# Attention on one NeuronCore: where V's product stands in the first step of a unit

## The chip, the cores and the metric

The kernel runs on one core of one Trainium2 chip. The metric is the device time in microseconds of one execution; three runs of the kernel before are shown. A profile covers one further execution. TensorE, ScalarE (ACT), VectorE (DVE), GpSimd (POOL) and SyncE (SP) run their own instruction streams and meet at semaphores.

## What is computed

```python
xn = _layernorm(x)                       # x: 2 x 1024 x 256, f32
x = x + attention(xn) + moe_ffn(xn)      # 8 experts, top 2

# attention: 16 heads of 16, 4 key heads
scores = einsum('bhqd,bhkd->bhqk', Qr, Kr) / HEAD_DIM ** 0.5
weights = softmax(scores, axis=-1)
out = einsum('bhqk,bhkd->bhqd', weights, V_rep)
return out.transpose(0, 2, 1, 3).reshape(b, s, d) @ W_o
```

All 1024 keys are seen by every query. Q and K are projected and turned by rope, the K heads are repeated four times over the query heads.

## The kernel before, in words

The first 170 us are the layer norm, the routing, the projections and the experts. Then comes the attention, in 16 units. A group g (0 to 7) is a batch and a key head; its unit u = 2 * g + h takes half h of the queries (512) for the four query heads of that key head. A unit has KT = 8 steps, kt = 0 to 7, one for each block of 128 keys.

For each step three streams work beside each other:

- **Scores, exponentials, V.** TensorE computes the scores of the next step (kt + 1) in two halves, j = 0 and j = 1, of two heads each (`scores`, L1338, matmuls at L1352; at kt = 0 of a unit a product that subtracts the maxima at L1348 goes ahead). Each half has one bank pair of PSUM, so half j of the next step waits until ScalarE has taken the exponential of half j of this step (`exp_done`). ScalarE's exponentials are at L785, two for each step, and each waits for its half (`st_ready`). V's product (`values`, L1356, matmuls at L1362) waits for both exponentials of its step and adds into the output bank over the eight steps. At kt = 0 it also waits for `o_free`: VectorE's transposition of that bank, L1080, which is issued after the maxima of the unit before.
- **Maxima of unit u + 2.** For the softmax of two units later TensorE computes four products of q and k for each step. Two go first, on rows 0 to 63 and 64 to 127 of the array (`score_first`, L1231 and L1233). The high keys' product (`score_high`, L1241) and the low keys' product (`score_low`, L1248) come later. ScalarE copies the result of L1231 out as the gain (`take_gain`, L736), in its queue behind the two exponentials of the step, and `score_low` waits for it, since it overwrites the bank. VectorE takes maxima: `take_a` (L992), `take_high` (L997) and `take_low` (L1003, merges the gain).
- **Side work.** VectorE transposes and inverts finished units (L1080, L1084, L1090) and prepares the maxima (L1009 to L1028). GpSimd divides (L649), mixes the experts' rows, and stages V (`stage_v`, L614). SP loads keys, queries and maxima for later groups.

Products on 64 rows are written out in pairs, a low one (rows 0 to 63) and a high one, which run beside each other. The order of TensorE is by hand. For steps 1 to 6, `values_between` (L1367) splits V into its first 128 and the other 384 query columns and puts two pairs between: scores half j = 1 of heads part 0 with `score_high`, then `score_low` with part 1. These are called the third and the fourth pair below; the first is `score_first` (the maxima pair), the second the scores of j = 0. For step 0, `values_behind` (L1376) puts third and fourth pair together and V whole behind them. Step 7 (L1444 to L1459) issues the scores of the next unit, `score_high` and `score_low`, and V whole. The last group (g = 7) has no maxima to compute and has a path of its own.

ScalarE's order in a step is: exponential j = 0, exponential j = 1, gain.

```python
def exps(u, first=False, ahead=True):
    for kt in range(KT):
...
        for j in range(2):
            act.wait_ge(st_ready, 2 * s + j + 1)
            act.activation(probs[kt % 2][:, 2 * j:2 * j + 2, :].rearrange("p r q -> p (r q)"),
                           st_ps[j][:, :], ACT.Exp, scale=1.0 / math.sqrt(HD)).then_inc(exp_done, 1)
        if ahead:
            take_gain(u + 2, kt)
```

Of the kernel before, what the change touches and what calls it, by code (L numbers as in the profile page):

```python
# [35 lines left out]
def build(nc, x, w_q, w_k, w_v, w_o, w_r, w_g, w_u, w_d, cos_t, sin_t, out):  # L36
# [3 lines left out]
    KV = w_k.shape[1] // HD  # L40
    R = NH // KV
    E, _, F = w_g.shape
    NT = B * S // P
    ST_T = S // P
# [27 lines left out]
    with ExitStack() as ctx:  # L72
# [297 lines left out]
        def max_bank(v, i):  # L370

            return first_mx_ps[i % 4] if v < 2 else mx_ps[(NI * v + i) % 3]
# [5 lines left out]
        def taken(v, n):  # L378

            return NTAKEN * v + n  # L380

        def key_block(kt):

            return kt // QT * QT + (3, 1, 2, 0)[kt % QT]
# [767 lines left out]
        def _(pe):  # L1152
# [72 lines left out]
            def score_first(v, q, p, k):  # L1225

                i, j, rows = 4 * k, k // QT, slice(k % QT * P, (k % QT + 1) * P)
                if v or k:
                    pe.wait_ge(mx_taken, taken(v, 3 * k - 1))
                low, high = max_bank(v, i), max_bank(v, i + 1)  # L1230
                mm(low.rearrange("p (c n) -> p c n", c=2), qs[q][0:STACK, j, rows], ka[p][0:STACK, :, QUART:HALF],  # L1231
                   start=True, stop=True).then_inc(mx_scored, 1)
                mm(high.rearrange("p (c n) -> p c n", c=2), qs[q][STACK:P, j, rows], ka[p][STACK:P, :, 0:QUART],  # L1233
                   start=True, stop=True).then_inc(mx_scored, 1)

            def score_high(v, q, p, k, waited=False):

                i, j, rows = 4 * k + 2, k // QT, slice(k % QT * P, (k % QT + 1) * P)
                if (v or k) and not waited:
                    pe.wait_ge(mx_taken, taken(v, 3 * k))  # L1240
                mm(max_bank(v, i).rearrange("p (c n) -> p c n", c=2), qs[q][STACK:P, j, rows], ka[p][STACK:P, :, QUART:HALF],  # L1241
                   start=True, stop=True).then_inc(mx_scored, 1)

            def score_low(v, q, p, k):

                i, j, rows = 4 * k + 3, k // QT, slice(k % QT * P, (k % QT + 1) * P)
                pe.wait_ge(gain_ready, STEPS * v + k + 1)
                mm(max_bank(v, i).rearrange("p (c n) -> p c n", c=2), qs[q][0:STACK, j, rows], ka[p][0:STACK, :, 0:QUART],  # L1248
                   start=True, stop=True).then_inc(mx_scored, 1)

            def score_second(v, q, p, k, waited=False):
                if (v or k) and not waited:
                    pe.wait_ge(mx_taken, taken(v, 3 * k))
                pe.wait_ge(gain_ready, STEPS * v + k + 1)
                score_high(v, q, p, k, True)
                score_low(v, q, p, k)
# [81 lines left out]
            def scores(q, v, p, kt, s, j, banks=None, parts=(0, 1)):  # L1338
                if s is not None and parts[0] == 0:
                    pe.wait_ge(exp_done, 2 * (s - 1) + j + 1)  # L1340
                out = [st_ps[j][:, i * HALF:(i + 1) * HALF] for i in range(2)]
                half = [slice(STACK * i, STACK * (i + 1)) for i in range(2)]

                first = ((0, 2, 3, 1), (3, 1, 2, 0))[kt // QT][kt % QT]
                keys = slice(first * P, (first + 1) * P)
                if kt == 0:
                    for i in parts:
                        mm(out[i], ones_r[half[i], :], ms[v][half[i], j, :], start=True, stop=False)  # L1348
                for i in parts:
                    if i == 1 and banks is not None:  # L1350
                        pe.wait_ge(mx_taken, banks)
                    last = mm(out[i], kb[p][half[i], kt // QT, keys], qs[q][half[i], j, :], start=False, stop=True, skip_group_check=kt > 0)  # L1352
                if parts[-1] == 1:
                    last.then_inc(st_ready, 1)

            def values(p, kt, s, u, columns=slice(0, HALF)):  # L1356
                if columns.start == 0:
                    pe.wait_ge(exp_done, 2 * (s + 1))
                    if kt == 0:
                        pe.wait_ge(o_free, u + 1)  # L1360
                for r in range(R):
                    last = mm(o_ps[32 * r:32 * (r + 1), columns], v_st[p][:, key_block(kt), :], probs[kt % 2][:, r, columns],  # L1362
                              start=(kt == 0 and columns.start == 0), stop=(kt == KT - 1), skip_group_check=True)
                if columns.stop == HALF:
                    last.then_inc(products_done, 1)

            def values_between(q, kv, p, kt, s, u, score):  # L1367

                values(p, kt, s, u, slice(0, P))
                scores(q, kv, p, kt + 1, s + 1, 1, None, (0,))  # L1370
                score_high(*score)
                score_low(*score)
                scores(q, kv, p, kt + 1, s + 1, 1, None, (1,))
                values(p, kt, s, u, slice(P, HALF))

            def values_behind(q, kv, p, s, u, score):  # L1376

                scores(q, kv, p, 1, s + 1, 1, None, (0,))
                score_high(*score)
                score_low(*score)  # L1380
                scores(q, kv, p, 1, s + 1, 1, None, (1,))
                if u % 2 == 0:
                    pe.wait_ge(v_staged, u // 2 + 1)
                values(p, 0, s, u)

            pe.wait_ge(kb_loaded[0], 128)
            pe.wait_ge(m_loaded[0], 64)
# [24 lines left out]
            def project(n, kt):  # L1412
                jobs = [(t, c) for t in out_tiles(n) for c in range(KC)]
                for t, c in jobs[len(jobs) * kt // KT:len(jobs) * (kt + 1) // KT]:
                    project_tile(t, [c])

            def group(g, p, last):
                for h in range(2):
                    u = 2 * g + h
                    ahead = 2 * (1 - p) + h  # L1420

                    for kt in range(KT):
                        s = KT * u + kt
                        if not last:
                            if kt == 0:
                                pe.wait_ge(q_loaded[ahead], 64 * ((g - p) // 2 + p) + 64)
                                if h == 0:
                                    pe.wait_ge(ka_loaded[1 - p], 128 * ((g - p) // 2 + p) + 128)
                            score_first(u + 2, ahead, 1 - p, kt)
                        if kt == KT - 1 and h == 0:  # L1430
                            pe.wait_ge(m_loaded[1], 64 * (g + 1))
                        if kt == KT - 1 and h == 1 and not last:
                            pe.wait_ge(kb_loaded[1 - p], 128 * ((g - p) // 2 + p) + 128)
                            pe.wait_ge(m_loaded[0], 64 * (g + 2))


                        if kt < KT - 1 and not last:
                            scores(2 * p + h, h, p, kt + 1, s + 1, 0)
                            if kt == 0:
                                values_behind(2 * p + h, h, p, s, u, (u + 2, ahead, 1 - p, kt))  # L1440
                            else:
                                values_between(2 * p + h, h, p, kt, s, u, (u + 2, ahead, 1 - p, kt))
                            continue
                        for j in range(2):  # L1444

                            free = taken(u + 2, 3 * kt) if j == 1 and not last else None
                            if kt < KT - 1:
                                scores(2 * p + h, h, p, kt + 1, s + 1, j, free)
                            elif h == 0:
                                scores(2 * p + 1, 1, p, 0, s + 1, j, free)  # L1450
                            elif not last:
                                scores(2 * (1 - p), 0, 1 - p, 0, s + 1, j, free)
                        if not last:
                            score_second(u + 2, ahead, 1 - p, kt, True)
                        if last:
                            project(h, kt)
                        if h == 0 and kt == 0:
                            pe.wait_ge(v_staged, g + 1)
                        values(p, kt, s, u)  # L1459

            for g in range(G):
                group(g, g % 2, g == G - 1)
# [37 lines left out]
```

## Time and profile before

| | us |
|---|---|
| median of three runs | 502.73 |
| lowest and highest | 502.05, 502.80 |
| the profiled execution, its own time | 502.22 |
| its span, first to last instruction | 500.3 |

The page gives the busy time of each engine, the granted TensorE clock (tenths of full speed, nine in all 40 slices, which is 90% or more; the mean over the core is 1.000), and the chain of work that ended last. The attention runs from about 171 to 492 us. Its steps are read in the timeline: start, duration, engine, line, operation, and in brackets the idle time of the engine before the row with what ended it. PE is TensorE's matmuls. The distance between the starts of two groups is a better measure of TensorE than the durations, as the ends are modelled.

### The profile page before, as it was taken

What the parts mean: (1) busy time and instruction counts of PE and PEld (TensorE: products, weight loads), DVE (VectorE), ACT (ScalarE), POOL (GpSimd) and SP (SyncE); (2) the same over time, 40 slices, a digit from 0 to 9 for tenths busy, and PEclk for the clock granted to TensorE, in tenths of its full rate; (3) what the DMA queues carried; (4) which work ended last, traced back from release to release, by engine and by line L of the source; (5) the groups of instructions that cost most, each with busy time, mean ns of one, the idle gap of its engine ahead of it and who ended that gap; (6) DMA issues with size and microseconds to landing.
All of it is one profiled execution on the core that took longest, in us unless ns stands there. A gap on an engine that the chain in (4) does not pass through costs nothing.

```text
span 500.3 us, 10998 instructions
## 1 busy us (share of the span) xinstructions
PE 490.1 (98%) x3952; PEld 266.7 (53%) x3952; DVE 371.7 (74%) x874; ACT 407.3 (81%) x551; POOL 172.2 (34%) x214
## 2 busy tenths in 40 slices
PE   7999999999999999999999999999999999999997
PEld 7836999888888633433333334333333343334433
DVE  4683867977876578788888887888888888884124
ACT  2646766665665699999999999999999999997772
POOL 5007677544521002241551426513454235400000
PEclk9999999999999999999999999999999999999999
DMA  8992467754573123122133024113223312001101
GB/s 286 370 313 62 111 208 233 205 174 154 135 208 88 66 66 87 42 65 88 45 88 104 24 68 137 32 45 98 76 63 88 86 44 61 27 3 33 43 33 63
DMA packets 41428, 52.76 MB, mean 105 GB/s; under 512 B 9792, under 2 KB 27584, under 8 KB 41376
## 3 DMA queue, kind: packets, MB, share of 16 engines
q1 hardware_dynamic: 29152, 34.36, 23.1%
q0 software_dynamic: 3408, 9.31, 7.2%
q10 hardware_dynamic: 8816, 8.40, 5.0%
q8 instruction: 32, 0.52, 0.4%
q14 instruction: 20, 0.16, 0.1%
HBM read 36.18 MB, written 15.60 MB: 104 GB/s over the span
## 4 chain that ended last, share of the span: by engine, by line
PE 94%; ACT 3%; DVE 2%; DMA 1%; issue 0%; ACTq 0%
PE bank L1362 28%; PE bank L1352 15%; PE bank L1292 14%; PE bank L1231 10%; PE bank L1302 7%; PE bank L1248 5%; PE bank L1407 3%; PE bank L1192 3%; PE bank L1284 2%; PE bank L1270 2%; ACT xn_t L736 2%; PE bank L1348 2%; PE bank L1181 1%; DMA xs<-in_L_attn_x 1%; PE bank L1196 1%; PE bank L1166 1%
## 5 line engine op out<-in xcount | busy, mean ns | idle before, releaser
L785 ACT ACTIVATE big<-bank 128x1024 f32<-128x1024 f32 x256 | 247.9, 1025 | 10.1 <-PE bank L1352 10.1
L1362 PE MATMUL bank<-big,v_st 128*32 128x384 f32 (+2 forms) x1696 | 154.3, 436 | 0.0
L1352 PE MATMUL bank<-qs,kb 64*128 64x512 f32 x512 | 133.9, 419 | 0.7 <-ACT big L785 0.7
L997 DVE TENSOR_REDUCE mx<-bank 128x1 f32<-128x512 f32 x128 | 87.9, 687 | 28.7 <-PE bank L1241 21.0
L992 DVE TENSOR_REDUCE mx<-bank 128x1 f32<-128x512 f32 x128 | 87.8, 686 | 15.6 <-PE bank L1233 13.5
L736 ACT ACTIVATE xn_t<-bank 128x512 f32<-128x512 f32 x128 | 76.4, 597 | 21.6 <-PE bank L1270 14.4
L1003 DVE CUSTOM_DVE_ANT_0 xn_t<-bank,xn_t 128x512 f32<-128x512 f32 x128 | 87.3, 682 | 0.0
L1352 PEld LDWEIGHTS bank<-qs,kb 64*128 64x128 f32 x512 | 63.9, 184 | 33.9 <-issue 16.7
L1292 PE MATMUL bank<-xn,work 128*128 128x128 f32 x624 | 76.0, 275 | 0.0
L1292 PEld LDWEIGHTS bank<-xn,work 128*128 128x128 f32 x624 | 72.9, 192 | 0.6 <-issue 0.5
L1362 PEld LDWEIGHTS bank<-big,v_st 128*32 128x32 f32 x1696 | 33.4, 108 | 68.8 <-issue 35.6
L649 POOL TENSOR_TENSOR xn<-xn,rden 128x256 f32<-128x256 f32 x15 | 9.5, 635 | 159.6 <-DVE rden L1084 144.4
L1231 PEld LDWEIGHTS bank<-ka,qs 64*128 64x128 f32 x112 | 20.5, 183 | 75.5 <-DVE mx L997 63.7
L1231 PE MATMUL bank<-ka,qs 64*128 64x512 f32 x112 | 55.4, 495 | 0.0
L1233 PE MATMUL bank<-ka,qs 64*128 64x512 f32 x112 | 55.3, 494 | 0.0
L1241 PE MATMUL bank<-ka,qs 64*128 64x512 f32 x112 | 52.9, 472 | 0.0
L1248 PE MATMUL bank<-ka,qs 64*128 64x512 f32 x112 | 45.7, 408 | 2.8 <-ACT xn_t L736 2.8
L569 POOL DMA_INDIRECT xn<-xn_d,token_of x39 | 40.2, 1030 | 20.2 <-PE bank L1284 13.0
L713 ACT ACTIVATE work<-big 128x1024 f32 x39 | 41.2, 1056 | 4.7 <-DVE slot_ei L979 2.9
L1302 PE MATMUL bank<-big,xn 128*128 x156 | 40.5, 382 | 0.3 <-DVE xn L1048 0.2
L634 POOL TENSOR_SCALAR rope_a<-rope_a,gate 128x256 f32<-128x256 f32 x32 | 29.3, 921 | 32.2 <-DMA rope_a<-rows_out,place_i 32.2
L1048 DVE SCALAR_TENSOR_TENSOR xn<-xn,bank 128x256 f32<-128x256 f32 x39 | 16.3, 419 | 31.4 <-ACT xn L749 31.3
(151 smaller groups left out, 534.3 us busy)
## 6 DMA issues: line engine op xcount, KB each, us to landing
qs<-q_hl SPq DMA_DIRECT2D x64, 128.0 KB, 2.8
rows_out<-xn ACTq DMA_DIRECT2D x37, 128.0 KB, 2.8
ka<-k_hl SPq DMA_DIRECT2D x64, 64.0 KB
kb<-k_hl SPq DMA_DIRECT2D x64, 64.0 KB
xs<-in_L_attn_x SPq DMA_DIRECT2D x4, 512.0 KB, 6.4
big<-in_L_ffn_Wg SPq DMA_DIRECT2D x16, 128.0 KB, 6.5
big<-in_L_ffn_Wu SPq DMA_DIRECT2D x16, 128.0 KB, 6.6
big<-in_L_ffn_Wd SPq DMA_DIRECT2D x16, 128.0 KB, 6.5
```

Source lines behind the costliest of these rows:

```text
L736: act.activation(gain[k % 2], max_bank(v, 4 * k), ACT.Relu).then_inc(gain_ready, 1)
L785: act.activation(probs[kt % 2][:, 2 * j:2 * j + 2, :].rearrange("p r q -> p (r q)"), st_ps[j][:, :], ACT.Exp, scale=1.0 / math.sqrt(HD)).t ...
L992: nc.vector.reduce_max(mx[h][:, STEPS + k, 0:1], max_bank(v, i), axis=X_AXIS).then_inc(mx_taken, 1)
L997: nc.vector.reduce_max(mx[h][:, STEPS + k, 1:2], max_bank(v, i), axis=X_AXIS).then_inc(mx_taken, 1)
L1003: nc.vector.tensor_tensor_reduce(larger, max_bank(v, i), gain[k % 2], scale=1.0, scalar=-FAR, op0=ALU.add, op1=ALU.max, accum_out=mx[h][:, ...
L1231: mm(low.rearrange("p (c n) -> p c n", c=2), qs[q][0:STACK, j, rows], ka[p][0:STACK, :, QUART:HALF], start=True, stop=True).then_inc(mx_sc ...
L1233: mm(high.rearrange("p (c n) -> p c n", c=2), qs[q][STACK:P, j, rows], ka[p][STACK:P, :, 0:QUART], start=True, stop=True).then_inc(mx_scor ...
L1248: mm(max_bank(v, i).rearrange("p (c n) -> p c n", c=2), qs[q][0:STACK, j, rows], ka[p][0:STACK, :, 0:QUART], start=True, stop=True).then_i ...
L1292: last = mm(gu_ps[i % 2][:, f * P:(f + 1) * P], w_now[i % 2][:, c, f * P:(f + 1) * P], rows_t[i % 2][:, c, :], start=(c == 0), stop=(c == ...
L1302: last = mm(y_ps[i % 2] if y is None else y, act_h[i % 2][:, c * P:(c + 1) * P], wdn[:, e, c, :], start=(c == 0), stop=(c == C - 1))
L1352: last = mm(out[i], kb[p][half[i], kt // QT, keys], qs[q][half[i], j, :], start=False, stop=True, skip_group_check=kt > 0)
L1362: last = mm(o_ps[32 * r:32 * (r + 1), columns], v_st[p][:, key_block(kt), :], probs[kt % 2][:, r, columns], start=(kt == 0 and columns.sta ...
```

## The change

Only the order in TensorE's stream at kt = 0 of the 14 units of groups 0 to 6 changes. V goes, whole, behind the third pair and ahead of the fourth, and the wait for the staged V goes with it. The function is renamed.

```diff
-            def values_behind(q, kv, p, s, u, score):
+            def values_within(q, kv, p, s, u, score):
 
                 scores(q, kv, p, 1, s + 1, 1, None, (0,))
                 score_high(*score)
-                score_low(*score)
-                scores(q, kv, p, 1, s + 1, 1, None, (1,))
                 if u % 2 == 0:
                     pe.wait_ge(v_staged, u // 2 + 1)
                 values(p, 0, s, u)
+                score_low(*score)
+                scores(q, kv, p, 1, s + 1, 1, None, (1,))
...
-                                values_behind(2 * p + h, h, p, s, u, (u + 2, ahead, 1 - p, kt))
+                                values_within(2 * p + h, h, p, s, u, (u + 2, ahead, 1 - p, kt))
```

## Rows read from the trace of the kernel before

**Rows 1.** The page: engine shares, and the chain that ended last by engine.
```profile
PE 490.1 (98%) x3952; PEld 266.7 (53%) x3952; DVE 371.7 (74%) x874; ACT 407.3 (81%) x551; POOL 172.2 (34%) x214
...
PE 94%; ACT 3%; DVE 2%; DMA 1%; issue 0%; ACTq 0%
```

**Rows 2.** Timeline of a regular step: start us, us, engine, line, operation, [idle before].
```profile
302.80 0.50 PE L1231 MATMUL bank<-ka,qs 64*128 64x512 f32 x1
303.14 0.39 PE L1352 MATMUL bank<-qs,kb 64*128 64x512 f32 x2
303.46 0.42 PE L1362 MATMUL bank<-big,v_st 128*32 128x128 f32 x8
303.81 0.50 PE L1352 MATMUL bank<-qs,kb 64*128 64x512 f32 x1
304.15 0.39 PE L1248 MATMUL bank<-ka,qs 64*128 64x512 f32 x1
304.48 0.85 PE L1362 MATMUL bank<-big,v_st 128*32 128x384 f32 x8
304.73 1.03 ACT L785 ACTIVATE big<-bank 128x1024 f32<-128x1024 f32 x1
305.26 0.49 PE L1231 MATMUL bank<-ka,qs 64*128 64x512 f32 x1
```

**Rows 3.** Timeline of a last step (kt = 7), TensorE alone.
```profile
311.23 0.40 PE L1352 MATMUL bank<-qs,kb 64*128 64x512 f32 x2
311.47 0.40 PE L1248 MATMUL bank<-ka,qs 64*128 64x512 f32 x1
311.80 1.07 PE L1362 MATMUL bank<-big,v_st 128*32 128x512 f32 x8
```

**Rows 4.** Timeline of the first step of the next unit, all engines.
```profile
311.26 1.94 ACT L785 ACTIVATE big<-bank 128x1024 f32<-128x1024 f32 x2
312.80 0.50 PE L1231 MATMUL bank<-ka,qs 64*128 64x512 f32 x1
313.11 0.71 DVE L1080 STREAM_TRANSPOSE xn<-bank 128x512 f32<-128x512 f32 x1
313.13 0.63 PE L1352 MATMUL bank<-qs,kb 64*128 64x512 f32 x3
313.25 0.18 PEld L1352 LDWEIGHTS bank<-qs,kb 64*128 64x128 f32 x1 [0.16 <-ACT big L785]
313.33 0.60 ACT L736 ACTIVATE xn_t<-bank 128x512 f32<-128x512 f32 x1
313.37 0.39 PE L1241 MATMUL bank<-ka,qs 64*128 64x512 f32 x1
313.82 1.94 ACT L785 ACTIVATE big<-bank 128x1024 f32<-128x1024 f32 x2
313.98 0.49 PE L1248 MATMUL bank<-ka,qs 64*128 64x512 f32 x1 [0.21 <-ACT xn_t L736]
314.40 1.06 PE L1362 MATMUL bank<-big,v_st 128*32 128x512 f32 x8
314.41 0.68 DVE L997 TENSOR_REDUCE mx<-bank 128x1 f32<-128x512 f32 x1
315.40 0.49 PE L1231 MATMUL bank<-ka,qs 64*128 64x512 f32 x1
315.43 0.69 DVE L1003 CUSTOM_DVE_ANT_0 xn_t<-bank,xn_t 128x512 f32<-128x512 f32 x1
315.93 0.60 ACT L736 ACTIVATE xn_t<-bank 128x512 f32<-128x512 f32 x1 [0.17 <-PE bank L1233]
316.06 0.42 PE L1362 MATMUL bank<-big,v_st 128*32 128x128 f32 x8
```

**Rows 5.** The gain copy (L736): who waited for it, us and times.
```profile
  PEld bank L1248: 7.3, 14
```

**Rows 6.** Timeline: TensorE's first row of another unit, four units earlier.
```profile
232.76 0.50 PE L1231 MATMUL bank<-ka,qs 64*128 64x512 f32 x1
```

## The prediction, made before the change was run

> **What bounds the kernel now.** I read the page first: engine shares and the chain that ended last [rows 1]. TensorE is busy 98% and carries 94% of the chain, most of it at the lines of the attention, ScalarE 81%, VectorE 74%. The granted clock is full in nearly every slice. That says TensorE, but the ends of matmuls are modelled, so a wait shorter than the overlap hides in a busy share. So the next view is the timeline of a regular step (kt from 1 to 6), read by the starts of TensorE's groups [rows 2]: first maxima pair 302.80, next pair j=0 303.14, V on 128 columns 303.46, third pair 303.81, fourth 304.15, V on 384 columns 304.48, next step 305.26. The distances 0.34, 0.32, 0.35, 0.34, 0.33, 0.78 add up to the step's 2.46 us.
>
> Is there a wait inside them? The pitch of V is 1.00 us for 512 columns (311.80 to 312.80) [rows 3, 4], 0.78 for 384 and 0.35 for 128: 0.22 for the first 128 columns removed and 0.43 for the next 256, so 0.22 per 128 columns and about 0.13 fixed. It grows evenly with the columns, so none of these is a wait. Pairs that follow each other stand 0.24 apart (311.23, 311.47) [rows 3]; the first pair after V takes 0.34 to the next, the last pair before V 0.33. Regular steps therefore run at TensorE's own pace. ScalarE follows with little room: two exponentials start 0.91 apart (1.94 for both [rows 4], 1.03 for one [rows 2]), and the gain copy takes 0.49 to the next start (313.33, 313.82) [rows 4]; 0.91 + 0.91 + 0.49 = 2.31 against 2.46.
>
> **The first step of a unit** (kt = 0) takes 2.60 (312.80 to 315.40) [rows 4], and there is a hole: the third pair starts at 313.37, the fourth at 313.98, 0.61 later instead of 0.24. It waits for ScalarE's gain, which itself started at 313.33, 0.53 after the maxima pair. The wait view has it 14 times, once for each unit that is not in the last group [rows 5]. This is what the edit goes for: it puts V (1.00 us) into that hole.
>
> **The change part by part.** Nothing is added or removed: V's matmuls, the two products, every semaphore count and DMA remain. V goes ahead of the fourth pair (the low keys' product, and the second half of the scores for kt = 1, j = 1). Three consequences.
>
> (1) The gain wait goes. The gain is done at 313.33 + 0.60 = 313.93, before the fourth pair can now come.
>
> (2) V waits for something else. It needs the exponentials of its step (end 311.26 + 1.94 = 313.20: there) and the free output bank, released by VectorE's transposition of the unit before, 313.11 + 0.71 = 313.82 [rows 4]. TensorE could start V at 313.37 + 0.33 = 313.70. From the end of a releasing instruction to the load it releases is 0.05 (exponential 313.20, load 313.25 [rows 4]), so V starts at 313.87: a new wait of 0.17. Bounds: 0 if V's wait overlaps otherwise, 0.27 if VectorE's release takes 0.1 more. I take 0.17, as the nearest release row says. The transposition itself does not move: it is queued on VectorE behind the unit before. The wait for the staged V costs nothing: staging is two groups ahead, with a whole group as cover (two units of 20.0 us, as below). Were it late, all of TensorE would stand, with the fourth pair now behind it.
>
> (3) The fourth pair comes late, and with it the second half of the scores for the next step. It starts at 313.87 + 1.00 = 314.87 instead of 313.98: 0.89 later. Who waits for it: ScalarE's second exponential of kt = 1. From the first pair after V to the ScalarE instruction that waits for it is 0.53 (315.40 to 315.93, a row marked as a wait for TensorE) [rows 4]. So it starts at 315.40 instead of 314.73, ends 1.03 later at 316.43, and V of kt = 1, which needs both exponentials, starts at 316.43 + 0.05 = 316.48. Before it started at 316.06 [rows 4]. **The unit is 0.42 longer.**
>
> The same from the slacks: the second exponential could have started at 313.98 + 0.53 = 314.51 and started at 315.76 - 1.03 = 314.73, slack 0.22; it ended at 315.76, plus 0.05 is 315.81 against V at 316.06, slack 0.25. Together 0.47 of cover for a shift of 0.89; 0.42 is left.
>
> TensorE's own pace would have V of kt = 1 earlier: after 314.87 come pairs at 315.21 and 315.45, V at 315.77. It then idles 0.71 for ScalarE, more than the 0.37 of the hole and its exposed load of 0.09 that went.
>
> What else moves: VectorE's merge with the low keys began at 315.43 and now could from 315.40, so it is covered, though by 0.03 only; a tenth more would delay the next maxima by as much, and they have spare time until the following maxima pair. The first maxima pair of kt = 1 comes at 315.21 and needs the high keys' maximum (314.41 + 0.68 + 0.05 = 315.14): free. No DMA and no work of SP or GpSimd is passed; their triggers (counts of score groups and products) shift by fractions of a microsecond beside transfers issued many steps ahead.
>
> Is 0.42 given back later in the unit? ScalarE has 0.15 spare per step, but the delay was already handed to TensorE at V of kt = 1, and TensorE has none: its step is the sum of its pitches. Continued: the gain starts 0.91 after 315.40, at 316.31, the next exponentials 0.49 later at 316.80 and end 1.94 later at 318.74; V of kt = 2 wants them at 316.48 + 2.46 = 318.94 by TensorE's pace. So TensorE paces again after a single step, and all engines are 0.42 late. The last step (kt = 7) shows no hole [rows 3] and hands over the same relative times, so the amount returns in each unit.
>
> The first unit has no unit before it to transpose; I price it like the others, 0.17 at most wrong. Units repeat: four take 80.04 (232.76 [rows 6] to 312.80 [rows 4]). So **14 x 0.42 = 5.9 us**. The last group has other code and only shifts.
>
> The profiled execution took 502.22 (span 500.3), 0.5 under the median 502.73; with 5.9 it gives 508.1, and the median forecast is 502.73 + 5.9 = **508.6**. The unit period goes from 20.0 to 20.4.
>
> **Where a rule of the skill stands.** The first pair after V and the last before it cost 0.10 and 0.09 more than the 0.24 of pairs in a row [rows 2, 3]. The edit makes a run of three pairs behind V (fourth pair, maxima pair, next pair), but the run ahead of V gets shorter by one: the number of V blocks is the same, so no such extra cost goes. The Trainium skill, "TensorEngine Tiling (Array Packing)", Key Properties, says that changing the tiling mode drains the engine; by that rule alone the edit would be worth nothing, since the changes of mode are as many as before. The trace agrees with the extra cost at each change, but has two other terms, the hole and the late scores.
>
> A second one bears on reading. The busy share of 98% shows neither the 0.61 nor the coming 0.71 as what they are. The Trainium skill, "Perfetto Trace Analysis", in the note that opens the page, calls matmul busy time a bad metric because matmuls are pipelined; the trace agrees, 0.61 between two starts appears as 0.21 idle [rows 4].
>
> **The rivals.**
> A, faster: only TensorE's instruction stream counts. Then V of kt = 1 stands at 315.77 instead of 316.06, 0.29 less, 14 x 0.29 = 4.1: 498.6. It needs the fourth pair to be late without cost, that is, shifted by no more than 0.47. For it: TensorE's 94% of the chain. Against: V alone puts 1.00 between the third and fourth pairs, where they stood 0.61 apart, and the second exponential's order in ScalarE's queue is fixed. Chance 0.05.
> B, no change: only changes of mode count, or ScalarE's 0.15 per step takes the delay back before TensorE feels it. For it: the spare time exists. Against: the wait falls in the very next step, before any can be taken back. 502.7, chance 0.04.
> C, slower by less: the bank is free when V wants it. V 313.70, all else 0.17 earlier: 0.25 per unit, 14 x 0.25 = 3.5: 506.2. Against: the transposition's end at 313.82. Chance 0.09.
> D, slower by more: the releases of V and of the exponential each take 0.1 longer than the rows I took them from, or VectorE's merge slips and its later maxima carry it: 0.62 per unit, 8.7: 511.4. Chance 0.08.
> My forecast has 0.74.
>
> **How the numbers follow.** 0.2% (about 1 us) is what a measurement of this kernel can tell from no change. Slower holds the forecast, C and D: 0.91; faster A: 0.05; same B: 0.04. The range runs from just below C (506.2 less 0.4, half of what the three runs shown span) to just short of D: 505.8 to 511.0; outside are A, B and most of D.
>
> **What would show it.** In the changed kernel: V of kt = 0 some 0.50 after the third pair, released by VectorE's transposition; the fourth pair 1.00 after V; a new idle time of ScalarE before the second exponential of kt = 1, of some 0.56 (315.40 less the end of the first, 313.82 + 1.02), 14 times; TensorE's V of kt = 1 starting 1.6 after the fourth pair, where pace alone gives 0.9; regular steps still 2.46. I am wrong if V's pitch there is well under 1.00, if the second exponential isn't late, or if the unit's period is 20.0 or less.

## The result: 7.5 us slower, and the profile after

| | before | after |
|---|---|---|
| median, five runs each | 502.73 | 510.19 |
| lowest and highest | 502.05, 502.80 | 509.70, 510.44 |
| profiled execution, span | 500.3 | 507.9 |

The ratio is 1.0153, with a 95% interval from 1.0143 to 1.0164: slower by 7.5 us, where 5.9 was forecast; 510.19 lies inside the range. On a further chip, told at the end of the experiments, the kernel before itself takes 511.3 us and the changed one 511.9: there the ratio is 1.0013.

The page of the changed kernel, shares and chain:

```profile
PE 487.7 (96%) x3952; PEld 266.7 (53%) x3952; DVE 372.6 (73%) x874; ACT 407.3 (80%) x551; POOL 171.7 (34%) x214
...
PE 86%; DVE 6%; ACT 4%; issue 3%; DMA 1%; DVEq 0%; ACTq 0%
```

Against [rows 1] TensorE's busy time is 2.4 us less over a span 7.6 longer, and its part of the chain falls from 94% to 86%. The other 8 points went to VectorE (2% before, 6% now: the transposition and the merge ahead of it), to time in which the profile shows no wait ("issue", 0% and 3%) and to ScalarE (3% and 4%): two waits have come into the chain. The timeline of a first step of the changed kernel, in the order of [rows 4] (the transposition's row is VectorE's):

```profile
316.69 0.50 PE L1231 MATMUL bank<-ka,qs 64*128 64x512 f32 x1
...
317.01 0.71 DVE L1080 STREAM_TRANSPOSE xn<-bank 128x512 f32<-128x512 f32 x1
...
317.27 0.39 PE L1241 MATMUL bank<-ka,qs 64*128 64x512 f32 x1
...
317.72 1.02 ACT L785 ACTIVATE big<-bank 128x1024 f32<-128x1024 f32 x1
317.84 0.19 PEld L1362 LDWEIGHTS bank<-big,v_st 128*32 128x32 f32 x8 [0.51 <-issue]
317.87 1.06 PE L1362 MATMUL bank<-big,v_st 128*32 128x512 f32 x8 [0.21 <-DVE xn L1080]
...
318.87 0.49 PE L1248 MATMUL bank<-ka,qs 64*128 64x512 f32 x1
...
319.20 0.39 PE L1231 MATMUL bank<-ka,qs 64*128 64x512 f32 x1
...
319.40 0.69 DVE L1003 CUSTOM_DVE_ANT_0 xn_t<-bank,xn_t 128x512 f32<-128x512 f32 x1
319.43 1.02 ACT L785 ACTIVATE big<-bank 128x1024 f32<-128x1024 f32 x1 [0.69 <-PE bank L1352]
319.43 0.40 PE L1352 MATMUL bank<-qs,kb 64*128 64x512 f32 x2
...
320.50 0.43 PE L1362 MATMUL bank<-big,v_st 128*32 128x128 f32 x8 [0.67 <-ACT big L785]
...
322.31 0.50 PE L1231 MATMUL bank<-ka,qs 64*128 64x512 f32 x1
```

Counted in us from the step's first row:

| | before | forecast | after |
|---|---|---|---|
| V of kt = 0 | 1.60 | 1.07 | 1.18 |
| fourth pair | 1.18 | 2.07 | 2.18 |
| second exponential of kt = 1 | 1.93 | 2.60 | 2.74 |
| V of kt = 1 | 3.26 | 3.68 | 3.81 |

Everything stands in the forecast's order and for its reasons: V waits for the transposition, the fourth pair comes 1.00 behind V, ScalarE is idle for 0.69 before the second exponential, V of kt = 1 waits for it. How often that happens stands in the views by line:

```profile
  PE bank L1352: 19.8, 30
...
  PE bank L1362: 9.5, 14
```

That is the view of ScalarE's exponentials (L785): their idle time for score halves, then who waited for them (us, times). In the kernel before, its first line reads:

```profile
  PE bank L1352: 10.1, 16
```

So there are 14 new waits of 0.69. V of kt = 1 waits for the exponential 14 times, 0.68 each. The same view of the transposition (L1080) in the changed kernel has V waiting for it 13 times, once in each of the 14 units but the first:

```profile
  PE bank L1362: 2.7, 13
```

Regular steps stayed at 2.46 (the step after the late V: 320.50 to 322.31 is 1.81, and 303.46 to 305.26 was 1.80 [rows 2]). Nothing was given back: units went from 20.0 to 20.5 or 20.6 (the first, in which V does not wait for the bank, from 20.91 to 21.40).

### The profile page after: what moved, and what is told of

Same layout as the page of the kernel before. It is cut to its first block, busy times and chain, and to the rows that moved or that the text cites. A ratio compares the mean times of both kernels' runs of the same rounds, so it can differ in the third digit from the quotient of the medians.

```text
span 507.9 us, 10998 instructions
## 1 busy us (share of the span) xinstructions
PE 487.7 (96%) x3952; PEld 266.7 (53%) x3952; DVE 372.6 (73%) x874; ACT 407.3 (80%) x551; POOL 171.7 (34%) x214
## 4 chain that ended last, share of the span: by engine, by line
PE 86%; DVE 6%; ACT 4%; issue 3%; DMA 1%; DVEq 0%; ACTq 0%
PE bank L1362 25%; PE bank L1352 14%; PE bank L1292 13%; PE bank L1231 7%; PE bank L1302 6%; PE bank L1248 6%; ACT big L785 3%; PE bank L1407 3%; PE bank L1192 3%; PE bank L1284 2%; PE bank L1270 2%; DVE xn_t L1003 2%; DVE xn L1080 2%; PE bank L1348 1%; PE bank L1181 1%
## 5 line engine op out<-in xcount | busy, mean ns | idle before, releaser
L785 ACT ACTIVATE big<-bank 128x1024 f32<-128x1024 f32 x256 | 249.7, 1026 | 19.8 <-PE bank L1352 19.8
L736 ACT ACTIVATE xn_t<-bank 128x512 f32<-128x512 f32 x128 | 76.4, 597 | 19.4 <-PE bank L1270 14.4
L1233 PE MATMUL bank<-ka,qs 64*128 64x512 f32 x112 | 54.0, 482 | 0.0
L1231 PE MATMUL bank<-ka,qs 64*128 64x512 f32 x112 | 54.0, 482 | 0.0
L1231 PEld LDWEIGHTS bank<-ka,qs 64*128 64x128 f32 x112 | 20.5, 183 | 63.7 <-DVE mx L997 52.8
L1241 PE MATMUL bank<-ka,qs 64*128 64x512 f32 x112 | 52.9, 473 | 0.0
L1248 PE MATMUL bank<-ka,qs 64*128 64x512 f32 x112 | 45.3, 405 | 0.0
```

Of the source, the lines that this page charges most:

```text
L736: act.activation(gain[k % 2], max_bank(v, 4 * k), ACT.Relu).then_inc(gain_ready, 1)
```

## Experiments

Theory 1 is the prediction's: the fourth pair carries the second half of the next step's scores, it comes late, ScalarE idles and holds V of kt = 1. Theory 2: the new wait for the output bank is what costs. Theory 3: only changes between V's blocks and the pairs count. Each diff is against the changed kernel unless it says otherwise.

### The scores ahead of V, alone

```diff
                 score_high(*score)
+                scores(q, kv, p, 1, s + 1, 1, None, (1,))
                 if u % 2 == 0:
                     pe.wait_ge(v_staged, u // 2 + 1)
                 values(p, 0, s, u)
                 score_low(*score)
-                scores(q, kv, p, 1, s + 1, 1, None, (1,))
```

> The second half of the next step's scores (part 1 of j = 1) goes ahead of V, alone, behind the third pair; only the low keys' product stays behind V. Theory 1 (the late scores idle ScalarE, which holds V of kt = 1): the bank wait stays, V still starts 1.18 after the step's first row, but the second exponential is on time. Then TensorE's pace counts: low keys' product at 2.18, maxima pair 2.51, next pair 2.75, V of kt = 1 at 3.07 against 3.26 before and 3.81 after the change: 0.19 x 14 = 2.7 us faster than the kernel before, about 500. Theory 2 (the wait for the output bank behind VectorE's transposition costs the time): nothing of it is removed, so it stays near 508 to 510. Theory 3 (only the runs of pairs between changes of mode count): no change against the kernel before, 502.7.

Measured: 500.7 us against 502.74 for the kernel before, ratio 0.9955 (0.9942 to 0.9969). Timeline of its first step:

```profile
312.54 0.50 PE L1231 MATMUL bank<-ka,qs 64*128 64x512 f32 x1
...
313.12 0.39 PE L1241 MATMUL bank<-ka,qs 64*128 64x512 f32 x1
...
313.35 0.40 PE L1352 MATMUL bank<-qs,kb 64*128 64x512 f32 x1
...
313.57 1.94 ACT L785 ACTIVATE big<-bank 128x1024 f32<-128x1024 f32 x2
...
313.72 1.06 PE L1362 MATMUL bank<-big,v_st 128*32 128x512 f32 x8
...
314.71 0.50 PE L1248 MATMUL bank<-ka,qs 64*128 64x512 f32 x1
...
315.60 0.43 PE L1362 MATMUL bank<-big,v_st 128*32 128x128 f32 x8
```

V stands where it does in the changed kernel (1.18), the bank's wait included, and the low keys' product too (2.17). Only the score half has moved, and the two exponentials of kt = 1 run back to back (1.94 for both, without idle time). V of kt = 1 comes at 3.06, forecast 3.07. One product moved takes 9.5 us off the changed kernel and makes it faster than the kernel before: Theory 1 holds, Theories 2 and 3 don't explain it. The product now runs without a partner, one more slot of 0.23, and still V fills the hole. Against the kernel before the gain is 2.0 where 2.7 was forecast: 13 units are 0.17 shorter (4.90 for their first two steps where it was 5.07), and the first unit, with 20.91 in both kernels, gains nothing.

### The bank free earlier, in both kernels

The transposition turns the first 32 of the 512 columns and leaves out the other 480, in all units but the last.

```diff
-                nc.vector.transpose(o_q, o_ps).then_inc(o_free, 1)
+                nc.vector.transpose(o_q[:, 0:32], o_ps[:, 0:32]).then_inc(o_free, 1)
```

> The changed kernel with VectorE's transposition of the output bank cut to its first 32 columns (of 512), so that the bank is free some 0.6 us earlier; 480 columns of each unit's output are left out, except in the last unit. Theory 1: V starts at 0.90 instead of 1.18 after the step's first row, everything behind it 0.28 earlier, V of kt = 1 at 3.53: 0.27 x 14 = 3.8 us over the kernel before, about 506.5. Theory 2: with the bank wait gone the loss is gone, 502.7 or less. Theory 3: unchanged against the changed kernel, 510.

> Control for the run above: the same cut of the transposition (480 of 512 columns of each unit's output left out, except in the last unit) in the kernel before. There V does not wait for it, so all theories say 502.7; if VectorE's own load mattered, it would be faster by up to 0.6 x 14 = 8 us.

Measured: 506.7 us in the changed kernel, ratio 1.0075 (1.0060 to 1.0091), and 502.82 in the kernel before, ratio 1.0000 (0.9991 to 1.0010). The first step of the former:

```profile
315.26 0.49 PE L1231 MATMUL bank<-ka,qs 64*128 64x512 f32 x1
...
315.58 0.21 DVE L1080 STREAM_TRANSPOSE xn<-bank 128x32 f32<-128x32 f32 x1
...
316.15 1.07 PE L1362 MATMUL bank<-big,v_st 128*32 128x512 f32 x8
...
317.14 0.50 PE L1248 MATMUL bank<-ka,qs 64*128 64x512 f32 x1
...
317.71 1.02 ACT L785 ACTIVATE big<-bank 128x1024 f32<-128x1024 f32 x1 [0.41 <-PE bank L1352]
```

V is at 0.89, the fourth pair at 1.88, and ScalarE still idles 0.41. The control says that VectorE's lighter load by itself is worth nothing. So of the 7.5 us the bank's wait is 3.5 (510.19 to 506.7, runs of two sets), and 4.0 stay without it. It adds to the delay of the scores; it isn't the cause by itself.

### V split, so that the fourth pair is less late

```diff
-                values(p, 0, s, u)
+                values(p, 0, s, u, slice(0, 256))
                 score_low(*score)
                 scores(q, kv, p, 1, s + 1, 1, None, (1,))
+                values(p, 0, s, u, slice(256, HALF))
```

The same was made with 128 and with 384.

> V of the first step in two parts, as in the steps behind it: 128 columns between third and fourth pair, 384 behind the fourth. Theory 1: V starts at 1.18 (bank), fourth pair at 1.53, the second exponential at 2.09 and done at 3.12, so it no longer decides; TensorE's pace does: 384 columns at 1.86, maxima pair 2.64, next pair 2.98, V of kt = 1 at 3.30 against 3.26: 0.04 x 14 = 0.6 us over the kernel before, about 503.3. Theory 2 (bank wait): near 510. Theory 3 (changes of mode): like the split at 256, 505 to 505.5.

> V of the first step in two parts: 256 columns between third and fourth pair, 256 behind the fourth. Theory 1: the fourth pair comes at 1.18 + 0.57 = 1.75 instead of 2.18, the second exponential starts at 2.31 and ends at 3.33, V of kt = 1 at 3.38 against 3.26 before: 0.12 x 14 = 1.7 us over the kernel before, about 504.4. Theory 2: V starts as early and waits for the bank as in the changed kernel, near 510. Theory 3: one more change of mode in each unit, 0.2 x 14 = 2.8 us more than the kernel before, 505.5.

> V of the first step in two parts: 384 columns between third and fourth pair, 128 behind the fourth. Theory 1: fourth pair at 1.18 + 0.78 = 1.96, the second exponential 2.52 to 3.55, V of kt = 1 at 3.60 against 3.26: 0.33 x 14 = 4.6 us over the kernel before, about 507.4. Theory 2: near 510. Theory 3: like the split at 256, 505 to 505.5.

| columns ahead of the fourth pair | expected | measured | ratio, 95% |
|---|---|---|---|
| 128 | 503.3 | 504.68 | 1.0035 (1.0022 to 1.0049) |
| 256 | 504.4 | 504.92 | 1.0043 (1.0027 to 1.0058) |
| 384 | 507.4 | 507.46 | 1.0092 (1.0076 to 1.0107) |
| 512 (the change) | | 510.19 | 1.0153 (1.0143 to 1.0164) |

From 256 columns on, each 128 cost 2.5 and 2.7 us, that is 0.18 and 0.20 in a unit, near the 0.22 that V takes for them. Theory 2 would have all at 510, Theory 3 all three alike: 384 and 512 speak against it. At 128 and 256 they are alike, and Theory 3's price of one more V block, 505 to 505.5, is closer there than Theory 1's 503.3 and 504.4. The kernel with 256 shows why the curve is flat below:

```profile
314.01 0.49 PE L1231 MATMUL bank<-ka,qs 64*128 64x512 f32 x1
...
317.43 0.43 PE L1362 MATMUL bank<-big,v_st 128*32 128x128 f32 x8
```

V of kt = 1 is at 3.42 and TensorE is not idle before it. ScalarE's wait is still there, 0.28, but it is no longer what V waits for: TensorE's own pace is.

The kernel with 384 has ScalarE's wait in between, 0.48 where the changed kernel has 0.69:

```profile
317.45 0.50 PE L1248 MATMUL bank<-ka,qs 64*128 64x512 f32 x1
...
318.02 1.03 ACT L785 ACTIVATE big<-bank 128x1024 f32<-128x1024 f32 x1 [0.48 <-PE bank L1352]
```

At 128 I missed by 1.4 us. Its first step:

```profile
314.45 0.49 PE L1231 MATMUL bank<-ka,qs 64*128 64x512 f32 x1
...
315.47 2.10 ACT L785 ACTIVATE big<-bank 128x1024 f32<-128x1024 f32 x2
...
315.63 0.43 PE L1362 MATMUL bank<-big,v_st 128*32 128x128 f32 x8 [0.22 <-DVE xn L1080]
...
315.98 0.50 PE L1248 MATMUL bank<-ka,qs 64*128 64x512 f32 x1
...
316.42 0.85 PE L1362 MATMUL bank<-big,v_st 128*32 128x384 f32 x8
...
317.20 0.50 PE L1231 MATMUL bank<-ka,qs 64*128 64x512 f32 x1
...
317.86 0.43 PE L1362 MATMUL bank<-big,v_st 128*32 128x128 f32 x8
```

The fourth pair to the second V block takes 0.44, where the expectation had 0.33. The fourth pair here is alone between two V blocks, so it pays both for being the first after V and for being the last before it: 0.24 + 0.10 + 0.09. V of kt = 1 is at 3.41 instead of 3.30, and 14 x 0.11 = 1.5 is the miss. TensorE's pace decides here too, not ScalarE, which has both exponentials in 2.10.

### Where V's waits stand

```diff
                 if columns.start == 0:
-                    pe.wait_ge(exp_done, 2 * (s + 1))
                     if kt == 0:
                         pe.wait_ge(o_free, u + 1)
+                    pe.wait_ge(exp_done, 2 * (s + 1))
+                    if staged is not None:
+                        pe.wait_ge(v_staged, staged)
```

(`staged` is the count that `values_within` used to wait for; that wait, in every second unit, goes last.) The same edit was made in the order with the scores alone ahead of V.

> The changed kernel, with the wait for the output bank first in V's waits instead of last. In the trace of the changed kernel the last waits stand in an instruction of their own on TensorE's queue, and V's weight load starts 0.115 after VectorE's transposition ends, its first matmul 0.03 later still; a load that carries its wait itself starts 0.05 after the release. If the place of the wait is what made this release dearer than I priced it, V starts 0.10 earlier and the time falls by 14 x 0.10 = 1.4 us to about 508.8. If releases by VectorE are slower whatever carries the wait, it stays at 510.2.

> The order with the second half of the scores alone ahead of V, and the wait for the bank first in V's waits. If the place of the wait matters, V starts 0.10 earlier; V of kt = 1 then waits for the second exponential, on time at 2.96 + 0.05 = 3.01 instead of TensorE's pace 3.06: 0.05 x 14 = 0.7 us less than that order alone, about 500.0. If it doesn't, 500.7.

Measured: 509.46, ratio 1.0133 (1.0118 to 1.0149), and 500.17, ratio 0.9946 (0.9932 to 0.9959). The medians moved by 0.7 and 0.5, where 1.4 and 0.7 were expected; the intervals of each pair overlap, so the runs alone don't settle it. The trace of the first does (V's product stands at L1364 there, by the added lines):

```profile
316.14 0.50 PE L1231 MATMUL bank<-ka,qs 64*128 64x512 f32 x1
...
316.47 0.71 DVE L1080 STREAM_TRANSPOSE xn<-bank 128x512 f32<-128x512 f32 x1
...
317.23 0.16 PEld L1364 LDWEIGHTS bank<-big,v_st 128*32 128x32 f32 x8 [0.45 <-DVE xn L1080]
...
318.80 1.02 ACT L785 ACTIVATE big<-bank 128x1024 f32<-128x1024 f32 x1 [0.61 <-PE bank L1352]
```

V's load starts 0.05 after the transposition ends (317.18) where it was 0.12 in the changed kernel (317.72 to 317.84), and the matmuls start with it, not 0.03 behind.

In the changed kernel's trace the wait for the bank is an instruction of its own ahead of the load, an EVENT_SEMAPHORE at L1360 from 317.76 to 317.81, which the timeline leaves out. The first wait in the program's order is the load's own, the others stand in the EVENT_SEMAPHORE. From the transposition's end to the load it is 0.114 to 0.115 in all 13 units of the changed kernel that wait for it, and 0.053 to 0.055 in all 13 here, in units with the wait for the staged V and without it, so that moved wait is not the reason.

V is at 1.09 instead of 1.18, and ScalarE's idle time is 0.61 instead of 0.69. In the second kernel TensorE reaches V at 1.13 by its own pace (312.97 after 311.84), since the lone product takes its slot; I had forgotten that bound, so 0.05 of the 0.10 is all there was:

```profile
311.84 0.49 PE L1231 MATMUL bank<-ka,qs 64*128 64x512 f32 x1
...
312.97 1.06 PE L1364 MATMUL bank<-big,v_st 128*32 128x512 f32 x8
...
314.86 0.43 PE L1364 MATMUL bank<-big,v_st 128*32 128x128 f32 x8
```

V of kt = 1 is at 3.02 against 3.06. This is the fastest version measured, 2.7 us below the kernel before.

### Another chip, where the kernel before is slower

To have the changed kernel and the one with the other order of waits side by side, both ran again.

> The changed kernel as it is, once more, as the partner of the run below on the same chip. 510.2, some 7.4 us over the kernel before (14 units longer by 0.53 to 0.55).

> The bank's wait first in V's waits, once more, beside the changed kernel on the same chip. By the units of the two traces (20.46 against 20.55) it is 14 x 0.09 = 1.2 us under the changed kernel. If the place of the wait doesn't matter, it is equal.

Measured: 511.92 and 511.20, and the kernel before 511.31 where it had been 502.7 to 502.9 in all earlier sets: ratios 1.0013 (1.0003 to 1.0023) and 0.9996 (0.9986 to 1.0007). This was another chip, and on it the kernel before is slower by 8.6 us. The two kernels differ by 0.7 once more, in the direction expected, where 1.2 was expected; these two intervals overlap as well. One further set on the same chip:

> The kernel before, with a profile. In the last pair of runs it took 511.3 where all others had 502.7, and the changed kernel only 511.9 where it had 510.2; the two traces taken there show single steps lengthened by 0.2 to 0.75, where the maxima pair's results reach ScalarE and VectorE late. If that chip gives such late results wherever it runs, a chip like it shows them here too, in steps of the kernel before, some 0.6 us in each unit in all; on a chip like the others this is 502.7 with every regular step at 2.46.

> The order with the second half of the scores alone ahead of V, beside the kernel before once more: 2.1 to 2.7 us faster on a chip like the first ones; on one with the late results, its gain is within their noise.

Measured: 509.84 for the kernel before (509.88 for its partner runs) and 504.23 with the scores alone ahead, ratio 0.9900 (0.9884 to 0.9917). The kernel before came out slow, as expected for such a chip. The other expectation missed: it had a gain within the noise here, and the gain is 5.6 us, more than the 2.0 elsewhere.

Mean length of a step over units 1 to 13, from the starts of the maxima pairs (a count over the whole trace, in us):

```
                        kt=0   kt=1   kt=2   kt=3   kt=4   kt=5
before                  2.61   2.46   2.46   2.46   2.46   2.46
before, this chip       2.61   2.47   2.94   2.56   2.48   2.50
after                   2.51   3.11   2.46   2.46   2.46   2.46
after, this chip        2.52   3.11   2.50   2.47   2.47   2.50
```

The two steps that the change touches are the same on both chips: 5.07 and 5.08 before, 5.62 and 5.63 after. What is added on this chip lies in kt = 2 to 5: 0.48 + 0.10 + 0.02 + 0.04 = 0.64 in a unit of the kernel before, 0.04 + 0.01 + 0.01 + 0.04 = 0.10 in the changed one; over these 13 units 8.3 and 1.3 us, against 8.4 and 1.3 between the spans (508.7 to 500.3, 509.2 to 507.9). Single steps are up to 1.1 longer. So the ratio of 1.0013 doesn't take the cost of the change in these two steps away; the kernel before has another loss there that the changed one mostly lacks. Why it lacks it isn't shown. Two places, the first from the kernel before, the second from the changed kernel with the other order of waits, where SP's loads of keys stand beside:

```profile
322.69 0.40 PE L1352 MATMUL bank<-qs,kb 64*128 64x512 f32 x2
322.88 0.60 ACT L736 ACTIVATE xn_t<-bank 128x512 f32<-128x512 f32 x1
...
323.77 1.94 ACT L785 ACTIVATE big<-bank 128x1024 f32<-128x1024 f32 x2 [0.29 <-PE bank L1352]
```

```profile
384.73 0.50 PE L1231 MATMUL bank<-ka,qs 64*128 64x512 f32 x1
...
385.00 3.13 SPq L451 DMA_DIRECT2D kb<-k_hl  x5
...
385.99 0.60 ACT L736 ACTIVATE xn_t<-bank 128x512 f32<-128x512 f32 x1 [0.79 <-PE bank L1233]
386.02 0.69 DVE L992 TENSOR_REDUCE mx<-bank 128x1 f32<-128x512 f32 x1 [0.90 <-PE bank L1233]
```

In the first, the scores are recorded as done at 323.09; ScalarE is through with the gain by 323.48 and then idles 0.29 for them. In the second, ScalarE takes the maxima pair 1.26 after its start, where 0.53 is usual (315.93 after 315.40 [rows 4]), and VectorE, which reads the other bank, takes it 1.29 after. So TensorE's results reach both readers late, in some units and not in others, while TensorE's next groups start at the usual distances (0.34, 0.32 and 0.36 in the second place). As the ends of matmuls are modelled, the trace can't say whether the products themselves take longer. What makes them late stays open: no run here changed the loads that stand beside, and I can't show that they matter. That it is the chip rests on two sets there against the sets on the others, taken at other times.

## Why the prediction was right, and what was mis-sized

- **What bounds the regular steps.** Right: 2.46 in both kernels, and the lateness isn't given back.
- **(1) The gain wait goes.** Right: no wait for L736 by the fourth pair is left.
- **(2) V waits for the bank.** The mechanism is right, the size of its last part, the release, was not. I took 0.05 from the end of the releasing instruction to V, from a load that carries its own wait. Here V starts 0.15 after it. The wait stands in an instruction of its own, because V has several waits, and the first one only is carried by the load: 0.12 to the load, 0.03 more to the matmul. The kernel with the bank's wait first got 0.09 of the 0.10 back. 14 x 0.10 = 1.4 us.
- **(3) The scores come late.** Right, and the larger part: forecast 0.53 from the fourth pair to the exponential, measured 0.56 (318.87 to 319.43). 14 x 0.03 = 0.4 us. Moving that one product back took the loss away.
- **The merge.** VectorE's merge with the low keys was to start no later than before. It starts 2.71 after the step's first row where it was 2.63, and delays nothing: the steps behind stayed at 2.46.
- **The sum.** 5.9 + 1.4 + 0.4 = 7.7 against 7.5 in the medians and 7.6 in the spans. Both misses have the same sign, so 510.19 lies 1.6 above the forecast, nearer to D's 511.4 and 0.8 under the range's upper end.
- **Rivals.** A (TensorE's stream alone counts) fell for this order; TensorE's pace decides in the splits at 128 and 256 and with the lone score half. B fell: ScalarE's spare time gave nothing back. C's condition (a free bank) didn't hold; made by experiment, it came out at 506.7, where C had 506.2. D, slower by more, named the dearer release, and part of it came true.
- **The rule on changing mode.** The kernel with 128 columns ahead, which has one more V block between pairs, shows the price: a pair between two V blocks takes 0.44 where a pair among pairs takes 0.24. "TensorEngine Tiling (Array Packing)", Key Properties, in the Trainium skill says that a change drains the engine; the trace agrees that each change costs, and the time of this edit came from elsewhere, as it leaves the number of changes as it was.

## What to carry to other kernels

Work that fills a wait also postpones what stood behind the wait: before moving it, list each product behind the gap with the engine that reads it next, and compare the shift (here 0.89 forecast, 1.00 measured) with that reader's slack (0.47). If only one product of several is urgent, send it ahead alone: an unpaired slot of 0.23 us in each unit took 9.5 us off the changed kernel here, and made it 2.0 us faster than the kernel before. And of several waits put the one that is likely to end last first in the program (worth 0.09 us at each place here), and measure on more than one chip before trusting one or two per cent.

## What I had not expected of the hardware

- The place of a wait among several changes when the work starts: 0.05 from release to load when the load carries the wait, 0.12 when another instruction does, with 0.03 more to the first matmul.
- One chip ran the same kernel 8.6 and 7.1 us (1.7% and 1.4%) slower in two sets at a granted clock of 1.0, with up to 1.1 added to single steps. How much is added differed from kernel to kernel: 8.4 us in the span before, 1.3 after, 3.2 where the scores go ahead alone (502.0 to 498.8), and 3.2 in the changed kernel with the other order of waits (510.0 to 506.8), one trace each.
